# A Fourier block on one core: row spectra copied from SBUF to SBUF in each step, and the MLP's raw weights loaded behind the last scatters

## The reference, cut to what matters

```python
# first layer
xn = layernorm(x, norm1_w, norm1_b)
xf = rfft2(xn, axes=(1, 2), norm='ortho')              # 32 x 17 complex frequencies
o1 = einsum('bhwni,hwnio->bhwno', xf, w1c) + b1c       # 8 blocks of 24 x 24, own weights for each frequency
o1 = complex(relu(o1.real), relu(o1.imag))
xs = irfft2(o1, s=(32, 32), axes=(1, 2), norm='ortho')
xm = layernorm(xs, norm2_w, norm2_b)
x  = xs + residual + gelu(xm @ mlp_w1 + mlp_b1) @ mlp_w2 + mlp_b2
# second layer: layernorm, 8 steps of a gated scan, layernorm, MLP
```

## Time and profile before

| | us |
|---|---|
| median of 3 runs | 1198.21 |
| lowest and highest | 1192.73 and 1200.53 |
| the profiled execution, its own time | 1196.19 |
| its span in the profile | 1194.4 |
| PE busy in the span | 1079.7 (90%) |
| DVE busy | 853.9 |
| ACT busy | 696.7 |
| POOL busy | 363.5 |

### The profile page before, as it was taken

How to read it: one execution, slowest core, us unless ns; L and a number is a source line. 1 busy time by engine, 2 the same in 40 slices (tenths; PEclk the granted TensorE clock), 3 DMA queues, 4 the chain that set the end, 5 groups by cost and what they waited for, 6 DMA issues and landing times. The chain is left out here.

```text
span 1194.4 us, 26159 instructions
## 1 busy us (share of the span) xinstructions
PE 1079.7 (90%) x9256; PEld 875.7 (73%) x9256; DVE 853.9 (71%) x2230; ACT 696.7 (58%) x1293; POOL 363.5 (30%) x383
## 2 busy tenths in 40 slices
PE   3659999985797999999799999999999699999998
PEld 1358888873486888888567767767677488888887
DVE  6645556442899988777768689689698767676665
ACT  3736556542664567666677567567545266766665
POOL 1250111211699200000238438338247311021110
PEclk9879999896898999999899999999999799999999
DMA  7888799896100000000100000000000000000001
GB/s 179 272 183 169 149 168 185 154 208 163 49 1 1 0 0 0 0 0 0 47 1 2 1 1 1 1 1 1 1 1 1 0 14 27 26 27 26 26 26 40
DMA packets 140186, 64.19 MB, mean 54 GB/s; under 512 B 115808, under 2 KB 134912, under 8 KB 140096
## 3 DMA queue, kind: packets, MB, share of 16 engines
q1 hardware_dynamic: 132888, 37.42, 15.5%
q0 software_dynamic: 5568, 18.73, 5.8%
q10 hardware_dynamic: 1648, 6.91, 1.8%
HBM read 44.17 MB, written 12.58 MB: 48 GB/s over the span
## 5 line engine op out<-in xcount | busy, mean ns | idle before, releaser
L904 ACT ACTIVATE L_conv_hf<-L_conv_ps,L_conv_b 128x512 f32<-128x512 f32 x192 | 132.1, 688 | 184.4 <-PE L_conv_ps L1075 175.7
L1094 PE MATMUL L_conv_ps<-w2hl,L_conv_hhi 128*128 128x384 f32 x768 | 229.2, 366 | 4.1 <-DVE X L990 4.1
L980 DVE TENSOR_TENSOR L_conv_hlo<-L_conv_hf,L_conv_hhi 128x512 fp32r<-128x512 f32 x192 | 140.9, 750 | 78.5 <-ACT L_conv_hhi L913 76.4
L1094 PE MATMUL L_conv_ps<-w2hl,L_conv_hlo 128*128 128x192 f32 x768 | 188.6, 252 | 0.0
L1209 POOL TENSOR_TENSOR sc_lo<-XS,sc_hi 128x512 fp32r<-128x512 f32 x96 | 142.9, 1504 | 116.1 <-ACT sc_hi L1285 116.1
L1487 PE MATMUL sc_ps<-sc_hi,wh 128*128 128x512 f32 (+1 forms) x440 | 160.8, 437 | 3.4 <-ACT XS L1269 3.2
L1094 PEld LDWEIGHTS L_conv_ps<-w2hl,L_conv_hhi 128*128 128x128 f32 x768 | 144.4, 188 | 8.7 <-DVE L_conv_hlo L980 3.4
L1487 PE MATMUL sc_ps<-sc_hi,wl 128*128 128x512 f32 (+1 forms) x440 | 147.8, 392 | 0.0
L1094 PEld LDWEIGHTS L_conv_ps<-w2hl,L_conv_hlo 128*128 128x128 f32 x768 | 146.2, 191 | 0.0
L636 PE MATMUL psF<-spectrum,X 100*24 100x64 f32 x4352 | 128.9, 290 | 15.2 <-issue 11.2
L861 POOL TENSOR_TENSOR X<-X,L_conv_b 128x192 f32 x128 | 83.2, 681 | 194.4 <-DVE L_conv_xn L964 194.4
(11 more groups left out here) (135 smaller groups left out, 2028.0 us busy)
## 6 DMA issues: line engine op xcount, KB each, us to landing
X<-in_L_conv_w SPq DMA_DIRECT2D x136, 144.0 KB
XS<-in_x POOLq DMA_DIRECT2D x8, 768.0 KB, 6.9
rows_spectrum<-XS POOLq DMA_DIRECT2D x8, 768.0 KB, 4.2
d<-rows_spectrum ACTq DMA_DIRECT2D x8, 768.0 KB, 5.5
X<-in_x SPq DMA_DIRECT2D x8, 768.0 KB, 8.2
out<-X SPq DMA_DIRECT2D x15, 384.0 KB, 2.6
XS<-d POOLq DMA_DIRECT2D x59, 96.0 KB, 4.7
spectrum<-in_L_conv_mlp_w SPq DMA_DIRECT2D x2, 576.0 KB, 9.3
```

Of the source, the lines that this page charges most:

```text
L904: nc.scalar.activation(hf[:, m % 3, :], ps[:, RB + m % 2, :], gelu, bias=b1[:, m:m + 1]).then_inc(act1, 1)
L980: nc.vector.tensor_tensor(hlo[:, m, :], hf[:, m % 3, :], hhi[:, m, :].bitcast(F32), ALU.subtract).then_inc(h_lo, 1)
L1094: mm = pe.matmul(o, x, w, start=(m == 0 and n == 0), stop=(m == MT - 1 and n == 1), skip_group_check=True)
```

## The change

In every step k, SP now copies the 16 partitions of group 0 and the 16 of group 1 straight from `d1` into `d2[0]` and `d2[1]`, two transfers of 96 KB. Before it issues them it waits for the step's four `d1_done` counts and for both copies of the step before. ACT, before it overwrites a `d1`, also waits for the copies of two steps before. POOL writes only the other 96 partitions to `F1` (576 KB in a step, not 768). ACT no longer waits for `f1_out` at the seam, nor reads groups 0 and 1 back; it has the `f1_out` wait before it reads group 2. The pieces of unit 0 are issued two at a time behind the copies of steps 4 to 7. Those of unit 1 wait for the last copy of group 1. At the other end of `fourier`, SP issues its three scatters first and the raw weights of the MLP behind them, without the waits on `mixed`.

```diff
-            for i in range(STEP):
-                sp.wait_ge(d1_done, 2 * TPB + 2 * i)
-                load_piece(0, i)
-            sp.wait_ge(d2_in[1], 16)
+            for k in range(TPB):
+                sp.wait_ge(d1_done, 4 * (k + 1))
+                for g in range(2):
+                    passed(sp, d2_in[g], 16 * k)
+                for g in range(2):
+                    sp.dma_start(d2[g][k:P:TPB, :, :].rearrange("p b c -> p (b c)"),
+                                 d1[k % 2][P // NG * g:P // NG * (g + 1)].rearrange("p b c -> p (b c)")).then_inc(d2_in[g], 16)
+                if k >= TPB // 2:
+                    for i in range(2):
+                        load_piece(0, 2 * (k - TPB // 2) + i)
+            sp.wait_ge(d2_in[1], 16 * TPB)
...
-            for n, (dst, src) in enumerate(sh.mlp_loads("L0_conv_")):
-                sp.wait_ge(mixed, STEP * (UNITS - 1) + n + 1)
-                sp.dma_start(dst, src).then_inc(sh.raw_in, 16)
             sp.wait_ge(d3_v, 2 * NG)
             sp.wait_ge(d3_a, 2 * NG)
             for k in (0, 3, 6):
                 scatter(sp, NG - 1, k)
+            for dst, src in sh.mlp_loads("L0_conv_"):
+                sp.dma_start(dst, src).then_inc(sh.raw_in, 16)
...
-                pool.dma_start(F1[:, k, :], d1[k % 2].rearrange("p b c -> p (b c)")).then_inc(f1_out[k % 2], 16)
+                late = slice(2 * P // NG, P)
+                pool.dma_start(F1[late, k, :], d1[k % 2][late].rearrange("p b c -> p (b c)")).then_inc(f1_out[k % 2], 16)
...
                         passed(act, f1_out[s], 16 * (k // 2))
+                        for g in range(2):
+                            passed(act, d2_in[g], 16 * (k - 1))
...
-            for s in range(2):
-                act.wait_ge(f1_out[s], 16 * TPB // 2)
-            for g in range(2):
-                spectrum_rows(g)
...
                         if u + 2 == last_of[g]:
+                            if g == 0:
+                                for k in range(2):
+                                    act.wait_ge(f1_out[k], 16 * TPB // 2)
                             spectrum_rows(g + 2)
...
-                pe.wait_ge(d2_in[g % 2], 16 * (g // 2 + 1))
+                pe.wait_ge(d2_in[g % 2], 16 * (TPB + g // 2))
```

## The result

The changed kernel takes 1201.16 us in the median of 20 runs (1193.85 to 1207.71); the kernel before, in 20 runs beside it, 1197.12 us (1190.28 to 1202.28). The ratio is 1.0045, with a 95% interval of 1.0028 to 1.0062: it is slower by about 5.4 us, clear of the interval though under one per cent. The prediction was 1192.0, with 1185 to 1198. The execution that was profiled has a span of 1198.7 us, against 1194.4.

The account below looks back on a forecast made before the run. It took PE as the bound from the first seam to 271 us, so time saved there arrives at the end. 1196.19 - 5.7 + 0 + 0 + 0.5 = 1191.0, or 1193.0 from the median; predicted 1192.0, range 1185 to 1198.

Parts of the forecast that it names:

- The seam's mechanism: First seam: SP's two last copies replace the `F1` write and read, PE starts at about 64.0 instead of 69.70, gain 5.7 us.
- The landing: First seam: time for a step 7 copy to land, taken from the scatters as 3.4 us, bounds 1.9 and 9.5.
- the wait for step 6's copies: Before the first seam: step 6's second copy starts at about 57.1, lands at 60.5 and then releases SP, later than 59.63.
- the prediction's own chain: First seam: step 6's second copy starts at about 57.1 and lands, then step 7's first copy lands and PE starts.
- its upper bound: First seam: with the longest scatter landing, 9.5 us, PE starts at or behind 69.2, a gain of 0.5 or less.
- The steps themselves: The eight steps: bytes per step stay the same, ACT and DVE set the pace; cost 0, up to 0.5 us.
- The moved MLP loads: Last unit and block end: the stall of 4.89 us stays, gain 0; the loads beside the DRAIN cost 0.5 us.
- rival 1: Last unit: the MLP loads held up the code, so the stall goes, saving 6.1 us: 1184.9, or 1186 to 1187; chance 0.13.
- the 0.5: Block end: the moved loads delay POOL's last scatter landing and its DRAIN by 0 to 5.3 us, taken as 0.5.
- rival 3: Block end: POOL's DRAIN grows with the loads, 5.3 us instead of 0.5: 1195.8 to 1197.8; chance 0.12.
- Rival 2: First seam: last copies land late, after 8 to 9.5 us, gain only 0 to 1: 1196 to 1198; chance 0.13.
- Rival 4: Eight steps: each step's copies wait for the last's, a loss from landings of 5.8 us; at 7, 1206 to 1208; chance 0.06.

Follow-up runs that it names:

- e9: The kernel before plus both copies a step with all the change's waits, but 12 KB each, groups 0 and 1 read back at the seam; 1196.56 us, ratio 0.9988.
- e13: The kernel before, but SP writes rows 0 to 31 of `F1` in two 96 KB transfers a step with the change's waits, POOL the rest; 1207.7 us, ratio 1.0083.
- e16: The kernel before plus one 96 KB copy a step (group 0) with its waits, `F1` written in full, both groups read back at the seam; one run, 1204.35 us.
- e3: The changed kernel, but POOL writes all 128 partitions of a step to `F1` again; 1200.55 us, ratio 1.0031.
- e4: The changed kernel with all eight weight pieces of unit 0 issued behind the last copies, none during the steps; 1202.37 us, ratio 1.0051.
- e10: The changed kernel with the copies issued by POOL ahead of its `F1` write; 1201.61 us, ratio 1.004.
- e11: The changed kernel with three `d1` tiles instead of two, so ACT waits for copies of three steps before; 1202.66 us, ratio 1.0052.
- e1: The changed kernel with the MLP loads back at their old place, so the copies alone; 1200.65 us, ratio 1.003.
- e2: The kernel before with only the MLP loads moved behind the last scatters; 1198.05 us, ratio 1.0011.
- e6: As e5, and each copy also writes 16 adjacent partitions of `d2` (output wrong); one run, 1203.16 us.
- e5: The changed kernel, but each copy reads every eighth partition of `d1` instead of 16 adjacent ones (output wrong); 1200.34 us, ratio 1.003.
- e17: The kernel before plus two 72 KB copies a step with the change's waits, `F1` written in full, seam as before; one run, 1199.08 us.
- e18: The changed kernel with each 96 KB copy made as two of 48 KB; 1199.09 us, ratio 1.0017.
- e14: The kernel before plus two 48 KB copies a step with the change's waits, seam as before; one run, 1207.3 us.
- e12: The kernel before, but groups 0 and 1 read steps 0 to 5 back early from `F1` and copy only steps 6 and 7; 1217.58 us, ratio 1.0186.
- e15: As e12, with `d2` ordered so the early read divides over 16 engines and later groups read in two parts; 1203.43 us, ratio 1.0055.

## Why the prediction was wrong, step by step

**The seam's mechanism was right, its size a factor of two off.** The write and the read of `F1` left the path, and SP's two last copies stood in their place. Predicted was a gain of 5.7 us; measured 2.8. Two terms were too small. The landing, taken from the scatters as 3.4, was 4.9 for the copy that PE waited for (74.01 to 78.95) and 4.7 in the median. And the wait for step 6's copies, taken as 1.0 us behind the last row copy (60.6 against 59.63), was 2.4 (74.01 against 71.64): the same mechanism, with the longer landing in it. By the prediction's own chain PE starts at 57.2 us plus two landings; with 4.7 that is a gain of 3.1, close to the measured 2.8. By the same chain its upper bound is wrong: a landing of 9.5 gives no gain of 0.5 but a loss of 6.5, since it counts twice.

**"The steps themselves" is the step that failed.** They were put at 0, up to 0.5, from two arguments. They measured +9.6 us in the two profiles and +7.6 in the means below. The first, "per step the bytes stay the same", is true and doesn't settle it. The 192 KB that changed hands went from a part of one 768 KB write to two transfers of 96 KB of their own, and the slabs and the write beside them land later (8.1 and 5.3 us, where it was 6.3 and 4.2). DVE waits for slabs 4 and 7, and PE's clock falls while it waits. e9 (no loss with the same waits and 12 KB a copy), e13 (the same loss into DRAM) and e16 (steps of 51.3 with one copy beside the full write) show that it is the transfers themselves; e3, e4, e10 and e11 shut out the cut write, the pieces, SP's queue and the depth of `d1` as the cause of most of it. By which way the transfers make the slabs late is not shown (see below). The second argument was that ACT and DVE set the pace behind a slab. They do only while the slab comes in time: DVE had waited for four slabs already, 0.99 us for slab 6, so there was little slack to lose.

**The sum.** The steps of the six kernels with all the copies whole and in place (changed, e1, e3, e4, e10, e11) have a mean of 53.3, those of the three without (before, e2, e9) 45.7: +7.6. The seams of the six have a mean of 7.1, those of before and e2 10.3: -3.2. Together +4.4; the mean ratio of the six is 1.0042, or +5.0 us. That these come so close is partly luck: e9's seam of 11.7 is left out, and the start of slab 1 and the stretch behind the seam differ between single profiles by several microseconds.

**The moved MLP loads** were rightly put at about nothing: e2 is within its interval of 1. The stall in the last unit stayed, so rival 1 is wrong: it was 3.20 to 6.51 us in the twenty kernels without relation to the move, among them 5.60 with it alone and 5.70 without it. The DRAIN stayed at 9.34 in the changed kernel, so the 0.5 was nothing as well, and rival 3 is wrong: 255 GB/s moved beside it. It was longer only in e10 (10.63) and e6 (10.42), and what sets it stays open.

```profile
284.00:286.00 2.00, 0.00 (x0) 0.00 (x0) 0.00 (x0) 0.00 (x0) 1.08 (x3) 0.78 0.98 255
```

**Rival 2** named the right symptom, a late copy, but put its price at the seam alone. Its sum is off as well: by the chain above a landing of 8 us is a loss of 3.5 at the seam, not a gain of 0 to 1. **Rival 4** had the right place and sign and the wrong mechanism: landings of 4.7 us are under its point of 5.8, and ACT waited for a copy once. Waits in a queue were asked after with care. What the new transfers do to others on the same 16 engines was asked only in bytes. (The prediction also says that PE waits for another engine once from 78 to 275 us; the waits list a second one, 0.3 us for DVE, which changes nothing.)

**What stays open.** By which way a copy of 96 KB makes the slabs late. The time for which the copies hold the 16 engines doesn't explain it: it was 4.0 us for eight copies in the changed kernel, 2.7 in e5 and at most 3.2 in e17, while the steps are 54.4, 52.5 and 45.4, and in the changed kernel the engines as a whole were less busy than before. How long a packet takes doesn't either, since e5's took less and its steps are hardly shorter. e18, with packets of half the bytes and the same bytes in all, has PE's time and clock as before, which speaks against the bytes as such; its own chain of copies hides the rest.

Nor does the median landing tell the fast kernels from the slow ones. In e17 slabs 4 and 5 took 7.4 and 8.5 us to land, about as long as in the changed kernel (8.1 and 8.1). What differs there is slab 7 and its neighbours. These are POOL's issues of slab 7 and of the next write of `F1`, first in the changed kernel, where the slab landed after 10.7 us, then in e17, where it landed after 6.9:

```profile
48.98 0.91 POOL L380 DMA_DIRECT2D XS<-in_x  x1 [1.47 <-ACT XS L415]
50.31 0.55 POOL L389 DMA_DIRECT2D rows_spectrum<-XS  x1 [0.43 <-ACT XS L426]
```

```profile
46.90 0.89 POOL L381 DMA_DIRECT2D XS<-in_x  x1 [2.19 <-DVE XS L529]
...
51.25 0.57 POOL L389 DMA_DIRECT2D rows_spectrum<-XS  x1 [3.46 <-ACT XS L426]
```

In all kernels with steps over 51 us a write of `F1` follows slab 7 within 2.7 us, and the slab lands in 7.8 to 11.0; in before, e2, e9, e14, e17 and e18 the write comes over 4 us behind, and the slab lands in 6.6 to 7.8. In e12 and e15, where no copy stands beside slab 7, the write follows within 1.7 us and the slab still lands in 7.4 and 7.1. So a small delay early in the steps may change which transfers meet later, copies among them, and that could make the jump. No run tests this. None of these versions beat the kernel before; e9's ratio has 1 within its interval, and it saves nothing by design.

## What to carry to other kernels

Don't take equal bytes for equal cost. Here 192 KB a step, taken out of a 768 KB write and sent as two transfers of their own, made steps of 45.7 us some 7.6 us longer, while 12 KB transfers in the same places cost nothing that could be measured. Before traffic is added to a loop that streams its input, look at whether the consumer already waits for that stream: there a later landing can be paid in full, and again where PE idles long enough that its clock falls. And follow a landing time through every place of the chain in which it stands; here it stood twice. The moved load, which no one waits for, made no measurable difference.

## What the runs showed of the hardware that was not expected

- In a transfer that moved alone a 6 KB packet took 0.24 us when 128 partitions were written out, 0.50 us from every eighth, 1.06 us from 16 adjacent ones; beside other traffic those of the copies took 0.50 us on average. Writing to 16 adjacent partitions didn't lengthen them (0.45).
- With two whole 96 KB copies from adjacent partitions in a step the slabs of 768 KB landed in 8.1 to 8.8 us in the median, instead of 6.1 to 6.3, although in the changed kernel the DMA engines were less busy in the steps than before (0.69 in place of 0.79).
- After idle times of PE of 3.7 and 6.3 us the copies behind its row matmuls came 1.28 us apart instead of 0.64, at a granted clock of 0.50, which is 1.2 in place of 2.4 GHz; before, the clock was at 0.50 behind an idle time of 3.2 us, too.
- POOL's DRAIN at the end of the block took 9.06 to 9.50 us in 18 of the 20 kernels, whether the MLP's loads moved beside it or not, and 10.42 and 10.63 in two.
- SP needed 2.4 us to issue four copies of 48 KB in e18, 0.6 each, as much as for one of 96 KB (1.13 us for two).
